# The feature layer with parts stationary and masks moving, and a reciprocal from ln, exp and one Newton step

## What is computed

```python
feat = softplus(x * (INV_SQRT2 * w0[0, 0]) + b0[0])
scores = feat * wa + ba
mask = adj > 0
logits = where(mask[None, :, :, None], scores[:, None, :, :], -1e9)
attn = softmax(logits, axis=2)
out = einsum('bijd,bjd->bid', attn, feat)      # then x = layernorm(x + out)
```

## Time and profile before

| | us |
|---|---|
| median of 3 runs (2281.03 to 2284.18) | 2282.41 |
| the profiled execution, device time | 2282.26 |
| its span, first to last instruction | 2280.4 |

### The profile page before, as it was taken

How to read it: one execution, slowest core, us unless ns; L and a number is a source line. 1 busy time by engine, 2 the same in 40 slices (tenths; PEclk the granted TensorE clock), 3 DMA queues, 4 the chain that set the end, 5 groups by cost and what they waited for, 6 DMA issues and landing times.

```text
span 2280.4 us, 54723 instructions
## 1 busy us (share of the span) xinstructions
PE 2047.9 (90%) x23604; PEld 1353.4 (59%) x23604; DVE 1714.9 (75%) x2077; ACT 1266.0 (56%) x2778; POOL 637.6 (28%) x503
## 2 busy tenths in 40 slices
PE   6999477776999579999999999999999999999993
PEld 5888367765888435556555556465555565555552
DVE  3999468994999566687787877877877877878763
ACT  3777544432677645664655655656556646555552
POOL 0233246653233200031231321312312313312214
PEclk8999779997999879999999999999999999999996
DMA  5000000000000000000000000000000000000000
GB/s 149 4 4 3 3 1 1 1 1 2 3 3 4 6 1 1 10 11 6 15 10 6 15 2 15 15 1 15 10 6 15 10 6 15 11 6 15 1 15 19
DMA packets 30783, 24.79 MB, mean 11 GB/s; under 512 B 21776, under 2 KB 25424, under 8 KB 30544
## 3 DMA queue, kind: packets, MB, share of 16 engines
q1 hardware_dynamic: 30544, 21.31, 3.9%
HBM read 8.72 MB, written 4.19 MB: 6 GB/s over the span
## 4 chain that ended last, share of the span: by engine, by line
PE 61%; DVE 2%; POOL 1%; ACT 0%; SPq 0%; issue 0%; DMA 0%; ACTq 0%; POOLq 0%; DVEq 0%
PE fourth_ps_out L1378 21%; PE fourth_ps_scores L1330 7%; PE fourth_ps_out L1392 5%; PE fourth_ps_scores L1333 5%; PE fourth_ps_scores L1336 5%; PE fourth_ps_prep L1298 3%; PE fourth_ps_prep L1306 3%; PE fourth_ps_prep L1291 3%; PE fourth_ps_scores L1354 2%; PE fourth_ps_scores L1360 1%; PE fourth_ps_scores L1357 1%; PE fourth_ps_scores L1363 1%; PE fourth_ps_prep L1281 1%; PE fourth_ps_prep L1259 1%; DVE fourth_weights L1030 1%; DVE fourth_mixed L1045 0%
## 5 line engine op out<-in xcount | busy, mean ns | idle before, releaser
L1030 DVE TENSOR_TENSOR fourth_weights<-fourth_weights,keep_mask 128x1024 f32<-128x1024 f32 x512 | 681.9, 1370 | 216.8 <-ACT fourth_weights L1178 215.2
L1178 ACT ACTIVATE fourth_weights<-fourth_ps_scores 128x512 f32<-128x512 f32 x1024 | 529.4, 605 | 422.6 <-PE fourth_ps_scores L1336 422.6
L1378 PE MATMUL fourth_ps_out<-fourth_weights,fourth_x_stage 128*64 128x512 f32 x2048 | 496.8, 605 | 0.0
L1378 PEld LDWEIGHTS fourth_ps_out<-fourth_weights,fourth_x_stage 128*64 128x64 f32 x2048 | 122.9, 136 | 233.0 <-issue 197.2
L1330 PE MATMUL fourth_ps_scores<-fourth_g_high,fourth_x_high 64*128 64x512 f32 x1024 | 230.4, 445 | 2.4 <-DVE fourth_g_low L989 2.4
L1330 PEld LDWEIGHTS fourth_ps_scores<-fourth_g_high,fourth_x_high 64*128 64x128 f32 x1024 | 96.7, 184 | 200.0 <-issue 105.5
L1185 ACT ACTIVATE fourth_weights<-fourth_ps_scores 128x1024 f32<-128x1024 f32 x128 | 125.2, 1026 | 142.9 <-PE fourth_ps_scores L1363 137.8
L1336 PE MATMUL fourth_ps_scores<-fourth_g_low,fourth_x_high 64*128 64x512 f32 x1024 | 203.5, 392 | 0.0
L1333 PE MATMUL fourth_ps_scores<-fourth_g_high,fourth_x_low 64*128 64x512 f32 x1024 | 203.1, 391 | 0.0
L1037 DVE TENSOR_TENSOR fourth_weights<-fourth_weights,keep_mask 128x1024 f32<-128x1024 f32 x128 | 153.2, 1238 | 66.1 <-ACT fourth_weights L1185 66.1
L426 DVE SCALAR_TENSOR_TENSOR first_weights<-first_ps_row,first_gain,keep_mask 128x1024 f32<-128x1024 f32 x128 | 159.3, 1267 | 2.5 <-ACT first_ps_row L527 2.5
(11 more groups left out here) (263 smaller groups left out, 3285.2 us busy)
## 6 DMA issues: line engine op xcount, KB each, us to landing
setup_adj<-in_adj SPq DMA_DIRECT2D x8, 512.0 KB, 7.3
fourth_h_high<-fourth_h_high SPq DMA_DIRECT2D x32, 128.0 KB, 2.3
fourth_h_low<-fourth_h_low SPq DMA_DIRECT2D x32, 128.0 KB, 2.3
out<-keep_x SPq DMA_DIRECT2D x16, 256.0 KB, 2.6
keep_x<-in_x SPq DMA_DIRECT2D x1, 512.0 KB, 11.6
fourth_bias_rows<-in_L_gnn_bh SPq DMA_DIRECT2D x8, 0.2 KB
fourth_wh_in<-in_L_gnn_Wh SPq DMA_DIRECT2D x2, 32.0 KB
fourth_wo_in<-in_L_gnn_Wo SPq DMA_DIRECT2D x1, 64.0 KB
```

What stands on the lines that cost most here:

```text
L1030: dve.tensor_tensor(buf[:, :], buf[:, :], keep.mask[:, st.t, :].bitcast(F32), ALU.mult)\
L1178: act.activation(weights[st.slot + g][:, cols(half)], ps_scores[g][:, cols(half)], ACT.Exp)\
L1378: last = pe.matmul(ps_out[rows(half), cols(g)], x_stage[st.s][:, st.t, half, :], weights[st.slot + g][:, cols(half)], start=(st.t == 0), s ...
```

## The change

In the setup keep.empty is multiplied by a column that is 1 on partitions 0 and 32 alone; the layers that read it have their means on partition 0.

In the feature layer each part of a source tile (128 sources x 128 columns: 64 products, 64 weights) is now the stationary operand, and 512 columns of the mask move. One bank per half of the nodes takes 4 tiles x 2 parts (`multiply_first`), 4 x 2 more (`multiply_last`) and one product with the totals. Both parts add up in the same bank, so that copy_rest and the sum of the parts fall away. The result lies with features on partitions: ScalarE copies it (`copy_turned`), TensorE turns it back by four transpositions (`turn_back`). ScalarE takes the log of the weights' sum and exp of minus that (`invert`), and VectorE makes of this near-reciprocal r, with w the sum of the weights and v that of the products, (w r - 2)(-v r) in three instructions (`divide`). The two parts of the totals lie on partitions 0 and 32 of one tile. The top is no longer widened on VectorE: a 64x1 instruction, then ScalarE scales the identity by it (`square_top`), and TensorE multiplies with ones stationary. Steps run to b = 17, the norm of batch b-2 is finished in step b, and the orders on all engines are new.

```diff
+                pool.memset(row_used[:, :], 0.0).then_inc(consts, 1)
+                pool.wait_ge(consts, 6)
+                for row in (0, LOW):
+                    pool.memset(row_used[row:row + 1, :], 1.0).then_inc(consts, 1)
+                pool.wait_ge(consts, 8)
                 pool.affine_select(out=keep.ident[:, :], in_=keep.ident[:, :], compare_op=ALU.not_equal, fill=1.0,
...
-                dve.tensor_scalar(keep.empty[:, :], degree[:, :], 0.0, None, ALU.is_equal).then_inc(empty_ready, 1)
+                dve.tensor_scalar(keep.empty[:, :], degree[:, :], 0.0, row_used[:, 0:1], ALU.is_equal, ALU.mult)\
+                   .then_inc(empty_ready, 1)
...
         def run_all(step):
-            for b in range(BATCH):
+            for b in range(BATCH + 2):
                 step(b, b % 2)
...
                 def residual(b):
-                    pool.wait_ge(count_ready, 4)
-                    pool.wait_ge(mixed_ready, BANKS * (b + 1))
+                    pool.wait_ge(mixed_ready, HALVES * (b + 1))
                     pool.tensor_tensor(norm.y[:, :, :], mixed[:, :, :], keep.x[:, b, :, :], ALU.add)\
                         .then_inc(norm.y_ready, 1)
-                    norm.centre(pool, b + 1)
                 def write_x(b):
-                    norm.inverse_deviation(pool, b + 1)
-                    pool.wait_ge(count_ready, 4)
                     pool.wait_ge(norm.rstd_ready, b + 1)
                     pool.tensor_tensor(keep.x[:, b, :, :], norm.centred[:, :, :], over_nodes(norm.rstd[:, :]),
                                        ALU.mult).then_inc(x_written, 1)
                 def step(b, s):
-                    if has(b - 1):
-                        residual(b - 1)
+                    if has(b - 2):
+                        norm.centre(pool, b - 1)
+                        norm.inverse_deviation(pool, b - 1)
                     if has(b + 1):
                         weigh_feat(b + 1, 1 - s)
+                    if has(b - 2):
+                        write_x(b - 2)
                     if has(b + 2):
                         score_nodes(b + 2, s)
                     if has(b - 1):
-                        write_x(b - 1)
+                        residual(b - 1)
                 score_nodes(0, 0)
                 weigh_feat(0, 0)
                 score_nodes(1, 1)
                 run_all(step)
-                residual(BATCH - 1)
-                write_x(BATCH - 1)
...
-                    wait(dve, wide_full, b)
-                    dve.scalar_tensor_tensor(out=top_wide[:, :], in0=bias_col[:, 0:1].to_broadcast([DIM, P]),
-                                             scalar=top[:, 0:1], in1=bias_col[:, 0:1].to_broadcast([DIM, P]),
-                                             op0=ALU.add, op1=ALU.subtract).then_inc(top_wide_ready, 1)
+                    wait(dve, square_ready, b)
+                    dve.tensor_scalar(top_biased[:, :], top[:, :], bias_col[:, 0:1], bias_col[:, 0:1], ALU.add,
+                                      ALU.subtract).then_inc(biased_ready, 1)
...
+                def divide(b, h):
+                    nodes = half_tiles(h)
+                    dve.wait_ge(back_full, HALVES * b + h + 1)
+                    dve.wait_ge(near_ready, HALVES * b + h + 1)
+                    dve.tensor_tensor(nearly_one[:, nodes, :], weights_of(h), near[:, nodes, :], ALU.mult)\
+                       .then_inc(one_ready, 1)
+                    dve.scalar_tensor_tensor(out=minus_mixed[:, nodes, :], in0=values_of(h), scalar=-1.0,
+                                             in1=near[:, nodes, :], op0=ALU.mult, op1=ALU.mult).then_inc(minus_ready, 1)
+                    dve.wait_ge(one_ready, HALVES * b + h + 1)
+                    dve.wait_ge(minus_ready, HALVES * b + h + 1)
                     wait(dve, norm.y_ready, b)
-                    dve.tensor_tensor(mixed[:, nodes, :], sums[:, nodes, 0:DIM], recip[:, nodes, :], ALU.mult)\
+                    dve.scalar_tensor_tensor(out=mixed[:, nodes, :], in0=nearly_one[:, nodes, :], scalar=2.0,
+                                             in1=minus_mixed[:, nodes, :], op0=ALU.subtract, op1=ALU.mult)\
                        .then_inc(mixed_ready, 1)
...
                 def step(b, s):
+                    if has(b - 2):
+                        norm.variance(dve, b - 1)
                     if has(b + 1):
                         find_top(b + 1)
                     if has(b - 1):
-                        norm.mean(dve, b)
+                        divide(b - 1, 1)
                     if has(b + 1):
                         shift(b + 1, 1 - s)
-                    divide(b, 0)
-                    if has(b + 1):
+                        lower_totals(b + 1, 1 - s)
                         split(b + 1, 1 - s)
-                    divide(b, 1)
-                    if has(b - 1):
-                        norm.variance(dve, b)
                     if has(b + 2):
                         find_tile_top(b + 2, s)
-                    if has(b + 1):
-                        lower_totals(b + 1, 1 - s)
-                    divide(b, 2)
-                    divide(b, 3)
+                    if has(b):
+                        divide(b, 0)
+                    if has(b - 1):
+                        norm.mean(dve, b)
...
+                def square_top(b):
+                    act.wait_ge(biased_ready, b + 1)
+                    wait(act, wide_full, b)
+                    act.activation(top_square[:, :], keep.ident[0:DIM, 0:DIM], ACT.Copy, scale=top_biased[:, 0:1])\
+                       .then_inc(square_ready, 1)
...
+                def copy_turned(b, h):
+                    act.wait_ge(out_full, HALVES * b + h + 1)
+                    wait(act, back_full, HALVES * (b - 1) + h + 1)
+                    act.activation(turned[:, half_nodes(h)], ps_out[h][:, :], ACT.Copy).then_inc(turned_ready, 1)
+                def invert(b, h):
+                    nodes = half_tiles(h)
+                    act.wait_ge(back_full, HALVES * b + h + 1)
+                    act.activation(logs[:, nodes, :], weights_of(h), ACT.Ln).then_inc(logs_ready, 1)
+                    act.wait_ge(logs_ready, HALVES * b + h + 1)
+                    wait(act, minus_ready, HALVES * (b - 1) + h + 1)
+                    act.activation(near[:, nodes, :], logs[:, nodes, :], ACT.Exp, scale=-1.0).then_inc(near_ready, 1)
                 def step(b, s):
+                    if has(b - 1):
+                        copy_turned(b - 1, 1)
+                    if has(b - 2):
+                        norm.square(act, b - 1)
                     if has(b + 2):
                         softplus(b + 2, s)
-                    copy_rest(b, 0)
+                    if has(b + 1):
+                        square_top(b + 1)
+                    if has(b - 1):
+                        invert(b - 1, 1)
                     if has(b + 1):
                         exp(b + 1)
                         round_weights(b + 1, 1 - s)
-                    copy_rest(b, 1)
-                    if has(b + 1):
+                        copy_totals(b + 1, 1 - s)
                         round_products(b + 1, 1 - s)
-                    if has(b - 1):
-                        norm.square(act, b)
-                    if has(b + 1):
-                        copy_totals(b + 1, 1 - s)
-                    copy_rest(b, 2)
-                    copy_rest(b, 3)
+                    if has(b):
+                        copy_turned(b, 0)
+                        invert(b, 0)
...
-                    pe.matmul(ps_wide[:, 0:DIM], top_wide[:, :], keep.ident[0:DIM, 0:DIM], start=True, stop=True)\
+                    pe.matmul(ps_wide[:, 0:DIM], keep.ones[0:DIM, :], top_square[:, :], start=True, stop=True)\
...
+                def multiply_first(b, s, h):
+                    if h == 0:
                         pe.wait_ge(rest_ready, b + 1)
...
+                    wait(pe, turned_ready, HALVES * (b - 1) + h + 1)
+                    for t in range(HALF_TILES):
+                        for part in range(2):
+                            pe.matmul(ps_out[h][:, :], parts[s][:, t, part, :], keep.mask[:, t, half_nodes(h)],
+                                      start=(t == 0 and part == 0), stop=False)
+                def multiply_last(b, s, h):
+                    for t in range(HALF_TILES, TILES):
+                        for part in range(2):
+                            pe.matmul(ps_out[h][:, :], parts[s][:, t, part, :], keep.mask[:, t, half_nodes(h)],
+                                      start=False, stop=False)
+                    pe.wait_ge(totals_low_ready, b + 1)
+                    pe.matmul(ps_out[h][:, :], totals[s][:, :], keep.empty[:, half_nodes(h)], start=False, stop=True)\
+                      .then_inc(out_full, 1)
+                def turn_back(b, h):
+                    pe.wait_ge(turned_ready, HALVES * b + h + 1)
+                    wait(pe, mixed_ready, HALVES * (b - 1) + h + 1)
```

(19 more changed lines are left out.)

106 lines of the change are left out of this document (45 added, 61 removed).

## The result

The changed kernel takes 2305.97 us (median of 4 runs, 2304.29 to 2308.16) against 2282.27 us before: 1.0104 times the time, 95% interval 1.0086 to 1.0121, or 23.7 us more. The forecast was 14.0 us more; its sign, its place and its mechanism came out, its size was 0.6 of the measured one.

A forecast was written before the change was run, and what follows sets the result against it. VectorE was taken to bound the kernel before, the norm's lap the changed one. Opening, 12 laps of 16.55 us and last steps end the layer at 556.4 against 542.40: 2282.3 + 14.0 = 2296.3 us, range 2280 to 2311.

The forecast's parts named there:

- VectorE bounds the kernel before: Feature layer before the change: VectorE, busy 13.1 to 13.5 us of a step of some 14.5, bounds the step.
- The edits by themselves: Busy times per changed layer step: VectorE 7.4 us, ScalarE 8.2, TensorE near 10.5; alone a gain of several us.
- The lap: Chain of orders and waits in the changed layer, from one norm's square to the next: 16.55 us against 15.15.
- The sum: Layer on the trace's clock: first square 325.0, 12 laps to 523.6, step 14 to 536.3, end 556.4; +14.0 us.
- Rival 1: In the layer, VectorE's split costs GpSimd nothing: lap 15.55 us, total 2283.3, no difference to tell; chance 0.13.
- Rival 2: Layer's lap through the norm does not close in one step; next lap 12.4 us, total 2246; 0.13 with smaller gains.
- Rival 3: In the layer, TensorE falls to 1.2 GHz for good: 2350 us, or 2310 in part; chance 0.08 with its parts.
- Rival 4: In the layer, VectorE stays full, near-reciprocal's three instructions taking 1.2 us each; time left as it is; chance 0.01.
- The rule of the Trainium skill: Certain VectorE instructions fully block against GpSimd reading SBUF; find_top's wait would cost 4.5 us over 13 steps, left out.

The follow-up runs named there:

- the run with the norm aside: Changed kernel, orders only: softplus one batch ahead, residual behind score_nodes, inverse deviation and write_x last on GpSimd, square and variance moved later; 2255.78 us, 0.9880 times the kernel before.

## Why the prediction was right, and where its size was off

*VectorE bounds the kernel before.* Right in the main, by the run without the reciprocal. That it had 13.5 us of work was too much: 2.5 of these were waits for GpSimd, and some of the pace of 15.15 came with the lower clock.

*The edits by themselves.* VectorE came to 7.7 us a step (7.4 forecast), ScalarE to 8.0 (8.2), the new instructions to 0.43, 0.41 and 0.43 us (0.41), the 64x1 top to 0.27 (0.15). TensorE came to 12.7 busy (10.5) at a clock of 0.90, and it is off the path (the run with half the products).

*The lap.* Right in every link and in their order; too short by 0.61 us. By the timeline above, counted from the square's end at 410.17:

| | forecast | measured |
|---|---|---|
| square_top starts | 2.50 | 2.50 |
| divide(b-1,1) starts | 3.46 | 3.64 |
| shift starts | 4.58 | 4.83 |
| weigh_feat starts | 5.97 | 6.26 |
| split ends | 9.34 | 9.63 |
| product ends | 11.82 | 12.15 |
| mean starts | 13.9 | 14.50 |
| next square ends | 16.55 | 17.17 |

0.18 are square_top (0.33 us long, its successor 0.23 later, where I had 0.12) and the longer exp; 0.07 and another 0.07 the two divides; 0.19 the tile top, which takes 1.09 us and passes on to the next instruction after 1.13, where I had taken 0.94. The other 0.1 us are gaps of 0.02 to 0.04 in the remaining links. The forecast's last link is also added up short: 13.9 and the 2.70 us of its own terms are 16.6, not 16.55.

*The sum.* The first square ended at 324.3 (325.0 forecast); 12 laps took 205.9 (198.6); step 14 took 13.2 (12.7); the rest 20.3 (20.1). -0.7 + 7.3 + 0.5 + 0.2 = 7.3 us, which is 563.65 - 556.4. The mis-sized term is the lap, 16.55 instead of 17.16, times 12. Another 0.85 us of the span's 22.1 lie behind the layer, and the medians are 1.6 us further apart than the spans; neither has a term in the forecast.

*Rival 1, split costs GpSimd nothing.* It fell: reading PSUM instead saved 1.1 us a lap.

*Rival 2, the lap through the norm is not in the way.* It fell for the changed kernel. Its figure for an open lap, 12.4 us, came near the 13.2 measured with the norm aside, but by luck: its lap leads through softplus and the copies, and the one that set the step leads through product, tile top, mean and find_top, with no softplus in it. What I had not seen is the branch beside softplus, and the mean that waits for write_x.

*Rival 3, TensorE at the lower clock throughout.* It fell: 0.90 granted, and without 16 of its 34 products a lap is 0.08 us shorter.

*Rival 4, VectorE stays full.* It fell: 7.7 us busy of 17.2.

*The rule of the Trainium skill* (SBUF — State Buffer, Who interferes with whom). The forecast had left out the 4.5 us that the rule would have put on the 64x1 tensor_scalar. In the timeline top_biased starts at 411.31, while the inverse deviation runs from 411.17 to 412.82, and takes 0.27 us: no wait. The section says that a tensor_scalar contends when its operands meet certain conditions; the forecast did not ask whether those of 64x1 do. The traces bear out the rule for some pairs and not for others. A tensor_scalar of 128x8 took 0.96 us in the run with the norm aside, until write_x was done, and two-input instructions of 64x128 and 128x128 waited beside GpSimd's 128x512 in the kernel before. The 64x1 took 0.27 us beside GpSimd's centring of 128x512 as well (414.67 in that run). And beside the inverse deviation of 128x8 not even an instruction with two SBUF inputs waited (divide's last in that run, 0.42 to 0.43 us in 13 steps). So both sides of a pair mattered here; what it is in them was not tested.

## What to carry to other kernels

When a change takes work from the engine that bounds a pipelined loop, follow the orders on all engines from one step to the same instruction of the next and add up that lap, because no busy time shows it: here 6 us of VectorE a step were saved and 2 were lost. A link that is cut out of a lap gives back only what separates it from the branch beside it (2.60 us of softplus gave 1.1 until the branch was moved too), and gives nothing once the lap is open. Then another lap sets the step, and it has to be followed in the trace anew: the one that had been priced ahead was not it. The layer norm of an earlier batch, which nobody needs soon, did best in this kernel where it stood behind what the next batch's products wait for. And where an instruction takes longer beside another engine's than alone, its busy time holds a wait.

## What the runs showed of the hardware

A ScalarE instruction of 64x64 takes 0.33 us, almost as long as one of 128x256 (0.36). A tile top of 128x512 on VectorE takes 1.01 to 1.02 us in most steps of the kernel before and 1.08 to 1.11 beside GpSimd's residual in the changed ones. With the steps at 12.65 us the clock stayed at 1.00 over TensorE's waits of 1.5 to 1.6 us, while at 13.2 us, with waits of 1.9 to 2.3 in most steps, it fell in some of them. Where one of VectorE's instructions runs into one of GpSimd's, either can pay: split took 1.32 us and feat 2.27 instead of 1.28, and the wide top of the kernel before 1.32 instead of 0.34.
